# Mixing each sample in its own half of TensorE's rows: 16 matmuls of 64x128 in place of 8 of 128x128

## The reference

```python
# attention part: adapters by sample, then an autocorrelation and the best delays
Bx = einsum('bni,bri->bnr', x, B[adapter_ids]); z = einsum('bnr,bor->bno', Bx, A[adapter_ids])
corr = irfft(rfft(z) * conj(rfft(z)))                # per row of z
weights, delay = top_k(corr, 6)
x = x + sum_k softmax(weights)[k] * roll(z, -delay[k])
# mixing: each sample's 64 rows are mixed by one of 16 matrices of 64x64
W = mix_weights[condition]                           # (64 samples, 64, 64)
m = einsum('bct,bcd->bdt', x, W)
# feed-forward: a base matrix, and two of eight low-rank experts by a router
combine = top-2 softmax of m @ W_router.T
x = x + m @ W_base.T + b_base + 2.0 * sum_e combine_e * (m @ A_e.T) @ B_e.T
```

## Time and profile before

| | |
|---|---|
| median of 3 runs | 855.38 us (853.22 to 855.9) |
| profiled execution | 851.39 us, its span 849.6 us |
| TensorE busy | 788.3 us, 93% |
| weight loads busy | 657.8 us, 77% |
| VectorE busy | 655.4 us, 77% |
| ScalarE busy | 328.2 us, 39% |
| GpSimd busy | 510.5 us, 60% |
| mean granted clock of TensorE | 0.969 of full speed |

### The profile page before, as it was taken

How to read it: one execution, slowest core, us unless ns; L and a number is a source line. 1 busy time by engine, 2 the same in 40 slices (tenths; PEclk the granted TensorE clock), 3 DMA queues, 4 the chain that set the end, 5 groups by cost and what they waited for, 6 DMA issues and landing times.

```text
span 849.6 us, 14441 instructions
## 1 busy us (share of the span) xinstructions
PE 788.3 (93%) x4828; PEld 657.8 (77%) x4828; DVE 655.4 (77%) x1387; ACT 328.2 (39%) x624; POOL 510.5 (60%) x447
## 2 busy tenths in 40 slices
PE   2967799999999999999999999999999999999897
PEld 2755678788878888788888888788878887877786
DVE  1256688988878787988878787988888788888952
ACT  3455344333543444333543444333533442333211
POOL 0123476757678766757677766757677664566621
PEclk9866799999999999999999999999999999999999
DMA  7769577887877888888877888887877877875521
GB/s 208 221 181 246 197 243 255 261 221 222 267 252 220 242 260 252 262 221 237 252 240 243 234 261 247 263 225 220 271 233 248 239 230 227 262 237 191 189 84 50
DMA packets 65661, 193.48 MB, mean 228 GB/s; under 512 B 13548, under 2 KB 23180, under 8 KB 62484
## 3 DMA queue, kind: packets, MB, share of 16 engines
q0 software_dynamic: 23040, 83.90, 33.9%
q1 hardware_dynamic: 31988, 72.93, 30.2%
q10 hardware_dynamic: 10560, 35.75, 10.8%
HBM read 117.82 MB, written 50.33 MB: 198 GB/s over the span
## 4 chain that ended last, share of the span: by engine, by line
PE 55%; POOL 15%; DVE 13%; issue 7%; DMA 5%; ACT 4%; SPq 1%; ACTq 1%; POOLq 0%; DVEq 0%
PE o_ps L502 27%; PE h_ps L640 5%; PE x_ps L526 5%; DMA y_d<-y 4%; PE c_ps L502 4%; POOL rolled L1266 3%; POOL turn L1289 3%; POOL eo L1293 3%; POOL row L1250 3%; PE t_ps L575 2%; PE t_ps L598 2%; PE x_ps L508 2%; ACT eo_hi L888 2%; PE x_ps L629 2%; POOL eo L1292 2%
## 5 line engine op out<-in xcount | busy, mean ns | idle before, releaser
L1266 POOL DMA_INDIRECT rolled<-y_d,off x160 | 203.9, 1274 | 218.2 <-DVE row L1073 105.2
L1073 DVE SCALAR_TENSOR_TENSOR row<-rolled,weight,row 128x1024 f32<-128x1024 f32 x160 | 222.1, 1388 | 10.2 <-DMA rolled<-y_d,off 3.9
L502 PE MATMUL o_ps<-wt_hi,x_hi 128*128 128x512 f32 x512 | 219.3, 428 | 0.0
L502 PE MATMUL o_ps<-wt_hi,x_lo 128*128 128x512 f32 x512 | 203.2, 397 | 0.0
L502 PE MATMUL o_ps<-wt_lo,x_hi 128*128 128x512 f32 x512 | 202.9, 396 | 0.0
L502 PEld LDWEIGHTS o_ps<-wt_hi,x_hi 128*128 128x128 f32 x512 | 97.4, 190 | 22.2 <-issue 4.6
L502 PEld LDWEIGHTS o_ps<-wt_hi,x_lo 128*128 128x128 f32 x512 | 96.4, 188 | 23.4
L502 PEld LDWEIGHTS o_ps<-wt_lo,x_hi 128*128 128x128 f32 x512 | 96.9, 189 | 15.7
L1250 POOL TENSOR_TENSOR row<-row,bias 128x1024 f32<-128x1024 f32 x32 | 77.7, 2427 | 16.3 <-PE x_ps L629 15.8
L849 ACT ACTIVATE turn<-t_ps 128x512 f32<-128x512 f32 x64 | 35.0, 596 | 101.5 <-PE t_ps L575 101.5
L1289 POOL TENSOR_TENSOR turn<-turn 128x256 f32<-128x256 f32 x64 | 71.7, 1141 | 2.6
(11 more groups left out here) (156 smaller groups left out, 1505.6 us busy)
## 6 DMA issues: line engine op xcount, KB each, us to landing
y_d<-y ACTq DMA_DIRECT2D x64, 512.0 KB, 3.6
row<-in_x SPq DMA_DIRECT2D x32, 512.0 KB, 7.7
out<-row SPq DMA_DIRECT2D x32, 512.0 KB, 6.1
adapter<-g_hi SPq DMA_DIRECT2D x62, 256.0 KB, 6.5
adapter<-g_lo SPq DMA_DIRECT2D x31, 256.0 KB, 6.7
r<-in_L_cond_A SPq DMA_DIRECT2D x60, 64.0 KB, 3.5
r<-in_L_cond_B SPq DMA_DIRECT2D x56, 64.0 KB, 5.9
rolled<-y_d,off POOLq DMA_INDIRECT x160, 7.1
```

Source lines behind the costliest of these rows:

```text
L502: last = pe.matmul(dst, a, b, start=start and n == 0, stop=stop and n == len(todo) - 1)
L1073: dve.scalar_tensor_tensor(rows[:, :], from_buffer[:, :], weight[:, n:n + 1], rows[:, :], ALU.mult, ALU.add).then_inc(sum_step, 1)
L1266: pool.indirect_dma_start(out=rolled[at % RB][:, :], out_offset=None, in_=y2_d[u], in_offset=bass.IndirectOffsetOnAxis(ap=off[s % 2][:, n: ...
```

## The change

`mixed` no longer multiplies with the whole 128x128 matrix. For each chunk it makes two matmuls, one for each sample `b`: partitions 64b to 64b + 63 of the rows (a stationary operand of 64x128) times the 64x64 block on the same partitions. The two results go to different banks: sample 0's eight chunks fill bank 0, and sample 1's bank 1, each of 64 columns a chunk. `x2_mm` is raised behind the last chunk of each sample, the last two matmuls of the sixteen. ScalarE and VectorE still take one bank a step, and write it to the same places of `x2`, `x2_hi` and `x2_lo` as before, which are now eight pieces of 64 columns. Since a bank no longer holds whole chunks, `project` and `base` wait for both banks ahead of chunk 0.

```diff
             def mixed(t):
                 pe.wait_ge(mix_in[t % NMIX], (t // NMIX + 1) * 32)
                 pe.wait_ge(sum_step, SUMS * t + SUMS)
+                rows, w = row[t % NROW], mix[t % NMIX]
                 for c in range(KC):
-                    last = pe.matmul(x_ps[:, c * P:(c + 1) * P], row[t % NROW][:, c * P:(c + 1) * P], mix[t % NMIX][:, :],
-                                     start=True, stop=True)
-                    if c % 4 == 3:
-                        last.then_inc(x2_mm, 1)
+                    for b in range(SPT):
+                        q, at = slice(b * C, (b + 1) * C), b * 512 + c * C
+                        last = pe.matmul(x_ps[:, at:at + C], rows[q, c * P:(c + 1) * P], w[q, q],
+                                         start=True, stop=True)
+                        if c == KC - 1:
+                            last.then_inc(x2_mm, 1)
 
             def project(t):
                 if t > 0:
                     pe.wait_ge(ht_l, t)
+                pe.wait_ge(x2_f, 2 * t + 2)
                 for c in range(KC):
-                    if c % 4 == 0:
-                        pe.wait_ge(x2_f, 2 * t + 1 + c // 4)
                     last = pe.matmul(h_ps[:, 0:HW], x2[:, c, :], aw[:, c, :], start=c == 0, stop=c == KC - 1)
...
             def base(t, c):
-                if c % 4 == 0:
-                    pe.wait_ge(x2_l, 2 * t + 1 + c // 4)
+                if c == 0:
+                    pe.wait_ge(x2_l, 2 * t + 2)
...
             def mixed_out(m):
-                for h in range(2):
-                    act.wait_ge(x2_mm, 2 * m + 1 + h)
-                    act.activation(x2[:, 4 * h:4 * h + 4, :].rearrange("p k r -> p (k r)"),
-                                   x_ps[:, h * 512:(h + 1) * 512], ACT.Copy).then_inc(x2_f, 1)
...
+                for b in range(SPT):
+                    act.wait_ge(x2_mm, 2 * m + 1 + b)
+                    of = x_ps[:, b * 512:(b + 1) * 512].rearrange("p (k r) -> p k r", k=KC)
+                    act.activation(x2[:, :, b * C:(b + 1) * C], of, ACT.Copy).then_inc(x2_f, 1)
+                    act.activation(x2_hi[:, :, b * C:(b + 1) * C], of, ACT.Copy).then_inc(x2_h, 1)
...
             def mixed_low(m):
...
+                for b in range(SPT):
+                    dve.wait_ge(x2_h, 2 * m + 1 + b)
+                    low(x2_lo[:, :, b * C:(b + 1) * C],
+                        x_ps[:, b * 512:(b + 1) * 512].rearrange("p (k r) -> p k r", k=KC),
+                        x2_hi[:, :, b * C:(b + 1) * C]).then_inc(x2_l, 1)
```

More of the change, by code:

```diff
@@ L891, in mixed_out @@
             def mixed_out(m):
-                for h in range(2):
-                    act.wait_ge(x2_mm, 2 * m + 1 + h)
-                    act.activation(x2[:, 4 * h:4 * h + 4, :].rearrange("p k r -> p (k r)"),
-                                   x_ps[:, h * 512:(h + 1) * 512], ACT.Copy).then_inc(x2_f, 1)
-                    act.activation(x2_hi[:, 4 * h:4 * h + 4, :].rearrange("p k r -> p (k r)"),
-                                   x_ps[:, h * 512:(h + 1) * 512], ACT.Copy).then_inc(x2_h, 1)
+                for b in range(SPT):
[3 more added lines that the diff above has]
+                    act.activation(x2_hi[:, :, b * C:(b + 1) * C], of, ACT.Copy).then_inc(x2_h, 1)
             def slot(s, u, i):
```

## The result

The changed kernel takes 872.52 us in the median of 4 runs (868.77 to 881.35), the kernel before 855.64 in its 4 runs on the same chip (853.22 to 856.09). The ratio is 1.022, with a 95% interval of 1.014 to 1.030: slower by 17 to 19 us, where 7.6 had been forecast. The profiled execution took 873.2 us with a span of 871.4, against 851.39 and 849.6, so 21.8 us of span are to be placed.

A forecast was written before the change was run, and what follows sets the result against it. TensorE was busy 93% of the span but held only 55% of the chain, so its time counts in some slots only. Terms 2.7 + 0.9 + 4.0 = 7.6 us on the median 855.38 gave 863.0; range 854 to 887.

The forecast's parts named there:

- Loads side by side: In the mixing on TensorE: loads for the two row halves run in parallel, 16 load times as now, +0.
- doubled speed: Rival: the mixing takes 0.9 us less; 854, no change (0.10), or 850.6 with a free mode change (0.05); chance 0.15.
- serial loads: Rival: the mixing's loads go one after the other, growing it by 1.79 + 0.18 us; 905 us; chance 0.15.
- half that: Rival: loads partly serial, half of that growth, about 1.1 us a mixing; 880 us; chance 0.06.
- Change of mode: TensorE's array mode around each mixing: +0.18 us going in, +0.20 going out; lower bound 0.
- Copies 1 us later: ScalarE's first copy comes over 1 us later after the mixing's start, since both banks are ready only at the last matmul.
- I cost this at 0: Seven slots without slack: VectorE's lateness, 0.7 us beyond TensorE's, falls in idle time behind; 0, uncovered 5 us.
- the 0.38 that was forecast: Mode change on TensorE in each of seven slots without slack, 0.18 + 0.20 us; 2.7 us in all.
- Middle kinds of slot: Slots where TensorE waits for `eo_lo`, with 0.46, 0.55 or 1.17 us to spare: entry and exit hidden, 0.
- two late slots: The last two of the fifteen slots with 0.46 or 0.55 to spare: chain through `x_lo` to MAX8, +0.46 each, 0.9 together.
- The two ends: Last two mixings, no correlation behind: `project` waits for both banks, +2.0 us each, uncovered, 4.0 together.

The follow-up runs named there:

- e3: The changed kernel with its loops exchanged: all eight matmuls of sample 0, then the eight of sample 1; 893.0 us, ratio 1.0477.
- e8: The kernel before, only that VectorE waits for both rounded copies before its first subtraction; 856.88 us, ratio 1.0031.
- e1: The kernel before with full-height mixing, but copies, `project` and `base` wait for both banks; 863.38 us, ratio 1.0138.
- e10: The changed kernel with GpSimd's bias added to 8 of 1024 columns only, part of the computation left out; 845.64 us.
- e0: The changed kernel again, no edit; 872.04 us, ratio 1.0224 to the kernel before.
- e4: The kernel before with late copies as in e1, but the last two mixings read bank by bank; 862.47 us, ratio 1.0106.
- e2: The kernel before with one extra 64x64 matmul in the lower rows ahead of each mixing, its result overwritten; 858.85 us, ratio 1.0081.
- e9: The kernel before with GpSimd's bias added to 8 of 1024 columns only, part of the computation left out; 832.19 us, ratio 0.9740.
- e7: The changed kernel with GpSimd's bias addition behind its first gather instead of its third; 894.29 us, ratio 1.0470.
- e5: The kernel before with the edits of e1 and e2 together; 876.29 us, ratio 1.0260.
- e6: The changed kernel with 16 useless matmuls between each of the last two mixings and its `project`; 870.6 us, ratio 1.0212.

## Why the prediction was right, and where it fell short

- **Loads side by side, +0**: right. 1.72 us from first to last start, against 1.67; serial (e3) it is 3.11. The Trainium skill (TensorEngine Tiling (Array Packing), Key Properties) has different tiles load and multiply in parallel, and with 0.055 against 0.100 us a load the runs agree. The doubled speed did not come. Loads of 128 columns follow each other at 0.112 us with 128 rows, at 0.100 with 64 rows and half the moving columns (e3) and at 0.11 with 32, so height buys hardly anything: the halves gave back what the doubled count took. The rivals of the serial loads (905), of half that (880) and of the doubled speed (850 to 854) are all out.
- **Change of mode, +0.18 in and +0.20 out**: nearly right, 0.10 in (391.08 to 391.41 less 0.23) and 0.22 more from mixing to correlation (1.93 against 1.71), 0.32 together.
- **Copies 1 us later**: right, 2.03 against 1.09 us behind the mixing's start, MAX8 0.93 later.
- **"I cost this at 0; with no cover it would be 7 x 0.7 = 5"**: this step failed. I had read two gaps in the slot behind, 0.37 us on VectorE and 0.86 on GpSimd, as cover. The timeline of VectorE and of GpSimd in the changed kernel's same slot, 14 us after the mixing:

```profile
405.58 2.71 DVE L1099 TENSOR_SCALAR rp<-rex,rinv 128x2 f32<-128x2 f32 x1
```

```profile
404.28 1.55 POOL L1267 DMA_INDIRECT rolled<-y_d,off  x1 [0.30 <-issue]
405.86 2.39 POOL L1251 TENSOR_TENSOR row<-row,bias 128x1024 f32<-128x1024 f32 x1
408.20 0.45 POOL L1286 TENSOR_TENSOR eo<-turn 1x128 f32<-1x128 f32 x1
```

  The gathers come later, so the bias addition starts 14.45 us after the mixing instead of 12.91, and VectorE's `rp`, which it holds, ends as late (GpSimd's row of before stands below). The late work then comes back to TensorE on two ways. First, by GpSimd: the 0.86 us before the powers are used up, and they begin as soon as the bias addition ends, 16.79 after the mixing instead of 16.32. From there to `eo_hi` it is 6.69 us instead of 6.21, so `eo_hi` is 23.48 behind instead of 22.53, and with it `eo_lo`, for which the next correlation waits. Second, by VectorE's `ht_lo`, which stands in its queue behind `rp` and two sums, and for which `experts` waits. VectorE, then the first matmul of `experts`, in the kernel before and in the changed one:

```profile
408.20 0.28 DVE L1014 TENSOR_TENSOR ht_lo<-h_ps,ht_hi 128x128 fp32r<-128x128 f32 x1
409.45 0.39 PE L502 MATMUL o_ps<-bs_hi,ht_hi 128*128 128x512 f32 x1
```

```profile
412.53 0.28 DVE L1015 TENSOR_TENSOR ht_lo<-h_ps,ht_hi 128x128 fp32r<-128x128 f32 x1
412.86 0.50 PE L502 MATMUL o_ps<-bs_hi,ht_hi 128*128 128x512 f32 x1
```

  Before, `ht_lo` was ready 0.97 us ahead of `experts` (0.3 in three of the six slots); now `experts` starts 0.05 behind its end. The slot has +0.93 from mixing to mixing, six times, 5.6 us. Half of it, 0.47, is TensorE's own (0.37 by which `base` starts later, 5.59 against 5.22, and 0.10 of the next entry): this is near the 0.38 that was forecast. The other half is what the text held for covered. e8 shows the same with TensorE's start as before: `experts` starts 0.05 behind `ht_lo`, and the slot has +0.5. Counted from a mixing to the next correlation, which is where `eo_lo` counts, the kernels follow VectorE's lateness: 0.59 gives 0.62 (e8), 0.89 gives 0.92 (e1), 0.93 gives 0.96. GpSimd's bias addition in the kernel before, from its timeline:

```profile
401.65 2.56 POOL L1250 TENSOR_TENSOR row<-row,bias 128x1024 f32<-128x1024 f32 x1
```

- **Middle kinds of slot, 0**: partly wrong. The 27 us slots did not move. Of the ten others before mixing 25, eight gained or lost up to 0.7, and two jumped (26.49 and 28.07 against 23.7). No term of the sum had such a jump. The row that would have warned was in the trace of before: one of 32 executions of L1065 at 4.05 us, a wait of 2.0 before L598, a clock fall behind it. The collisions themselves did not become more: counted on the timeline, in 7 slots of before an operation of VectorE ahead of `s_t` is caught by the bias addition (L1060 six times, L1065 once), in 8 of the changed kernel (three and five). What grew is how often and how long TensorE has to wait for `s_t`, 2 times to 4 and 2.1 us to 9.1. Without the bias collision (e10) 5.6 us of the change's price go. Of the two late slots for which the sum had +0.46 each, one did not grow (23.03 against 23.04), and the other grew by 1.75 with the clock fall at 820.4 in it.
- **The two ends, +2.0 each**: the mechanism and its size are right (3.75 against 3.8 worked out; e1 has +1.9 at full clock), but each cost 3.6 to 3.7 in the profiled execution, because a clock fall stood behind both; in e0 it stood behind one (3.6 and 1.9). I had priced the wait and not the work behind it.

By the sum: 7.6 forecast, 17 to 19 measured. The sign, the mixing itself and the change of mode were right, and so were the kinds of cost at the ends. The size was less than half, because lateness in the steady part was put down as covered: lateness alone costs 11.8 (e1), some 9 of it steady (e4). That 872.5 still lies in the stated range is in part luck. The forecast by itself was given 858 to 868; the range went up to 887 for the sake of half-serial loads at 880, which did not happen.

Two readings of the prediction are a little off, without weight in the sum: of the seven distances given as 2.88, six are 2.96; and the 0.11 us that a matmul is said to take besides its load is not shown by a row (256 moving columns of the one-pass type go at 0.12, so 128 may take 0.06; added to the load that is still over the 0.112 seen, and the overlap stands).

**What stays open.** Of the 13.5 us that are left with a short bias addition, 12.1 are in the profiles, and some 7.9 of them have a cause (2.3 in the slots and 5.6 at the ends, one clock fall among them). The others are +2.7 in the five slots behind those, -0.7 and +1.1 in the ten after them, and +1.2 in mixings 25 to 30; what made them is open. Which of the two ways back to TensorE would cost how much without the other was not tried either. Why e2 costs 6.9 rather than 4 to 5 is argued from its three held executions of L1066, not tried. How many clock falls a run has differs between the traces of the same kernel (e0 and the first one differ in place), and each of the other kernels has one profile, so their share of the 19 us can't be given. No kernel here that computes the whole result beat the one before.

## What to carry to other kernels

Count the loads before splitting the array: where a float32 matmul with few moving columns is paced by loading its weights, two half-height tiles side by side need twice the loads and end at the same time, and any order in which both results are finished together takes from the readers the head start on the first one. What this costs depends on who reads them. When a step makes an engine later, do not take an idle gap in the next slot as cover until you have followed the late work through every queue to the next wait of the bound engine, and looked at the slowest execution of each operation, not at its median: one of 32 at three times its length is a collision, and a small delay can use up what covers it. Price a new wait on TensorE with the lower clock that may follow it: of the waits of 1.75 to 3.1 us in the changed kernel's first trace some had it behind them and some not.

## What the runs showed of the hardware

- Two float32 operations of VectorE are held for about as long as GpSimd adds two 128x1024 float32 tensors. L1066: 1.28 us alone, 4.14 beside the addition of 2.39; L1099, a tiny one, 0.23 alone in e10 and 2.71 beside it. By the profile L1066 had begun 0.66 us before the addition and was held all the same. With the addition cut to 0.2 us in the median (e9) no L1065 is over 1.35. The Trainium skill (GPSIMD Engine Reference, section 1. Specifications) says that the two engines share their interface to SBUF and names as contending the VectorE operations with two SBUF inputs or in a two-port mode. L1066 reads two tensors of SBUF, which agrees with it. L1099 reads one and a scalar, and whether it ran in a two-port mode no trace shows. That they are held nearly to the addition's end or past it, the runs add.
- Two half-height tiles of TensorE load side by side when the instructions alternate, 0.055 us a load, and not in two blocks of 16, 0.100.
- A wait of 1.75 us behind the split mixing was followed by the lower clock, both times in the first trace of the changed kernel. Behind the full-height mixing of e1, with the same wait, it was not. The windows of e1 there:

```profile
823.40:825.10 1.70, 0.03 (x1) 0.06 (x1) 0.64 (x1) 1.70 (x4) 1.70 (x1) 1.00 0.81 333
825.10:827.10 2.00, 2.00 (x17) 2.00 (x18) 0.74 (x2) 0.31 (x1) 0.65 (x1) 1.00 0.04 14
827.10:829.10 2.00, 2.00 (x10) 1.59 (x9) 1.83 (x6) 0.39 (x2) 0.00 (x0) 1.00 0.00 0
```

  In the traces of the changed kernel, e0, e7 and e10 together it fell behind 5 of 8 such mixings, and in e1 and e5, with the mixing of full height, behind none of 4. The steady part says the same: where the correlation waits 0.8 us or more for `eo_lo` behind a split mixing, the clock fell within 0.6 us of the correlation's start in 4 of 14 places (one in the first trace of the changed kernel, two in e0, one in e6, none in e10); behind a mixing of full height (before, e1, e4, e8, e9) in none of 27. So the split mixing probably has this price of its own besides lateness and mode. No experiment changed that alone, and e5, whose mixing is of full height, is no faster for it, so this is a strong hint and not shown.
